# A two-layer decoder on one core: attention work reordered, two heads a PSUM bank in cross attention, MoE gathers four tiles ahead

## Reference

```
x = x + causal_attention(norm(x))            # 16 heads of 16, rotary positions
x = x + cross_attention(norm(x), context)    # 16 heads, 120 keys
x = x + PEER(norm(x))                        # product-key experts, top 10 of 8 heads
x = x + banded_attention(norm(x))            # 0.1 added to scores within 2 of the diagonal
x = x + BiDAF(norm(x), context)              # attention both ways, then W_l
x = x + MoE(norm(x))                         # 8 experts 256 -> 1024 -> 256, top 2
```

## Time and profile before

| | us |
|---|---|
| median of 3 runs | 4062.17 (4061.87 to 4063.05) |
| profiled execution | 4071.27 |
| its span, first to last instruction | 4069.5 |
| causal attention | 0 to 519 |
| cross attention | 519 to 930 |
| PEER | 930 to 2599 |
| banded attention | 2599 to 3112 |
| BiDAF | 3112 to 3389 |
| MoE | 3389 to 4069 |

### The profile page before, as it was taken

How to read it: one execution, slowest core, us unless ns; L and a number is a source line. 1 busy time by engine, 2 the same in 40 slices (tenths; PEclk the granted TensorE clock), 3 DMA queues, 4 the chain that set the end, 5 groups by cost and what they waited for, 6 DMA issues and landing times. The chain is left out here.

```text
span 4069.5 us, 98588 instructions
## 1 busy us (share of the span) xinstructions
PE 3425.7 (84%) x33488; PEld 2849.1 (70%) x33489; DVE 2980.0 (73%) x11747; ACT 1109.9 (27%) x2400; POOL 1658.6 (41%) x1626
## 2 busy tenths in 40 slices
PE   6999858784899988889999999777786886799998
PEld 4777635444788888888888888555554666688887
DVE  6778646667999999999999999499995444433332
ACT  1333424442222222222222222154442111122221
POOL 3223122212666666666666667532320000233332
PEclk8999968876999999999999999899997886799999
DMA  5344344432000000000000000244441005466665
GB/s 148 100 113 106 82 112 111 112 83 93 2 2 3 2 2 2 2 2 2 2 2 2 2 2 2 65 107 104 107 105 32 7 7 173 131 168 168 169 171 130
DMA packets 256580, 278.71 MB, mean 68 GB/s; under 512 B 43841, under 2 KB 200641, under 8 KB 255713
## 3 DMA queue, kind: packets, MB, share of 16 engines
q1 hardware_dynamic: 242401, 254.81, 22.1%
q0 software_dynamic: 13824, 19.18, 3.1%
HBM read 188.88 MB, written 72.42 MB: 64 GB/s over the span
## 5 line engine op out<-in xcount | busy, mean ns | idle before, releaser
L1129 POOL TENSOR_TENSOR peer_hot_v<-peer_hot_e,peer_parts 80x512 bf16<-80x512 bf16 x768 | 1038.1, 1378 | 505.0 <-DVE peer_hot_e L1168 504.1
L974 PE MATMUL peer_ps_u<-peer_up,peer_g 128*128 128x256 f32 x2048 | 547.9, 416 | 0.6 <-DVE x_all L1285 0.6
L955 PEld LDWEIGHTS peer_ps_h<-peer_xnT,peer_down 128*128 128x128 f32 x4096 | 511.6, 197 | 15.6
L955 PE MATMUL peer_ps_h<-peer_xnT,peer_down 128*128 128x128 f32 x4096 | 510.1, 279 | 0.0
L965 PE MATMUL peer_ps_w<-peer_hot_v,peer_hot_u 80*128 80x32 bf16 x12288 | 347.7, 177 | 177.1 <-DVE peer_g L1180 94.1
L965 PEld LDWEIGHTS peer_ps_w<-peer_hot_v,peer_hot_u 80*128 80x128 bf16 x12288 | 335.3, 97 | 204.0 <-DVE peer_hot_u L1172 109.4
L974 PEld LDWEIGHTS peer_ps_u<-peer_up,peer_g 128*128 128x128 f32 x2048 | 407.8, 208 | 55.6 <-issue 1.0
L1052 ACT ACTIVATE peer_g<-peer_ps_h 128x512 f32<-128x512 f32 x256 | 152.9, 597 | 901.9 <-PE peer_ps_h L955 901.9
L1172 DVE TENSOR_TENSOR peer_hot_u<-peer_count,peer_uvT 80x2048 bf16<-80x2048 bf16 x256 | 344.8, 1347 | 0.0
L1940 PE MATMUL moe_ps_t<-moe_xgT,moe_w 128*128 128x128 f32 x2304 | 275.3, 278 | 0.0
L1998 POOL DMA_INDIRECT moe_xg<-moe_xn_rows,moe_source x72 | 71.5, 993 | 485.7 <-DVE moe_target L2099 451.2
(11 more groups left out here) (353 smaller groups left out, 6874.2 us busy)
## 6 DMA issues: line engine op xcount, KB each, us to landing
moe_w<-in_moe_w SPq DMA_DIRECT2D x144, 512.0 KB, 4.9
causal_qs<-causal_qscratch SPq DMA_DIRECT2D x32, 384.0 KB, 3.8
cross_qs<-cross_qscratch SPq DMA_DIRECT2D x32, 384.0 KB, 3.6
band_qs<-band_qscratch SPq DMA_DIRECT2D x32, 384.0 KB, 3.9
moe_w<-in_moe_w SPq DMA_DIRECT2D x8, 1024.0 KB, 9.5
causal_qscratch<-causal_part SPq DMA_DIRECT2D x32, 192.0 KB, 2.0
causal_kscratch<-causal_part SPq DMA_DIRECT2D x32, 192.0 KB, 2.0
causal_ks<-causal_kscratch SPq DMA_DIRECT2D x32, 192.0 KB, 4.3
```

Source lines behind the costliest of these rows:

```text
L955: mm = nc.tensor.matmul(ps_h[:, n % 2, k * P:(k + 1) * P], down[:, c, 4 * n + k, :], xnT[:, par, c, :], start=(c == 0), stop=(c == DC - 1))
L974: mm = nc.tensor.matmul(ps_u[:], g[:, par, v, :], up[:, v, :], start=(v == 0), stop=(v == EV - 1))
L1129: ins = nc.gpsimd.tensor_tensor(hot_v[0:SEL, n % RING, part], hot_e[0:SEL, n % RING], w, ALU.mult)
```

## The change

In attention there are 16 probability buffers instead of 8, so that ScalarE waits for the weighing of the batch before and not for that of the same batch. Weighings come two steps later (steps 7, 11 and 15, and 3 of the next macro), the sums at 4, normalise at 7, the output projection at 11. The norm of a batch is made at step 13, three batches ahead, and the second half of `stack` stands before `turn_max` and waits only until the old heads have been read. In cross attention two heads share a PSUM bank: one instruction of VectorE and one of ScalarE treats both.

BiDAF's SyncE stores finished x tiles to the output; the MoE stage stores the last four only. In MoE there are four `xn` buffers, the w2 loads are issued behind all xn stores, the tables are made four columns at a time, there are 71 tiles and not 72, ScalarE copies the gates out of `xg`, and gathers are issued four tiles ahead and wait for `xgt_used`.

```diff
+    G = 2 if cross else 1
+    WIDE = 512 // G
...
-        probT = sb("probT", [P, 8, COLS])
+        probT = sb("probT", [P, HEADS, COLS])
...
-        PROJECT, OUT, VALUES, STACK = (2, 4, 6, 8), 10, 12, 10
-        NORMALISE = 5
+        PROJECT, OUT, VALUES, STACK, NORM = (2, 4, 6, 8), 11, 12, 10, 13
+        WEIGH, SUMS, NORMALISE = 7, 4, 7
...
                 if s > 0:
                     e.factor(b, par, s - 1)
                 if s == 0:
+                    if there(b + 1):
+                        e.stack(b + 1, 1 - par, 1)
                     if there(b - 1):
                         e.turn_max(b, par, 1)
-                    if there(b + 1):
-                        e.stack(b + 1, 1 - par, 1)
                 if there(b - 1):
-                    if s == 1:
+                    if s == WEIGH - 4:
                         e.weigh(b - 1, 1 - par, NQUAD - 1)
-                    if s == 2:
+                    if s == SUMS:
                         e.sums(b - 1, 2 * b + 2)
                     if s == NORMALISE:
                         e.normalise(b - 1, 1 - par)
-                if s % 4 == 1 and s > 1:
-                    e.weigh(b, par, s // 4 - 1)
+                if s >= WEIGH and s % 4 == WEIGH % 4:
+                    e.weigh(b, par, (s - WEIGH) // 4)
+                if s == NORM and there(b + 3):
+                    e.norm(b + 3)
                 if there(b + 2):
-                    if s == 0:
-                        e.norm(b + 2)
                     if s == 1:
                         e.turn(b + 2, par)
...
+            e.norm(2)
...
-                    settle(parts_out, OUTS * (b + 1))
+                    if c == 0:
+                        settle(parts_out, OUTS * (b + 1))
+                    else:
+                        settle(s2_done, HEADS * (b - 1))
...
-                    wait(pe, nmax_ready, HEADS * b + h - 1)
+                    if h % G == 0:
+                        wait(pe, nmax_ready, HEADS * b + h - G)
                     for q in range(TT):
                         c0, n = qcol[q], seen[q]
-                        mm = nc.tensor.matmul(ps_1[:, h % 2, c0:c0 + n], qs[0:ROWS, par, h, q * P:(q + 1) * P],
+                        mm = nc.tensor.matmul(ps_1[:, h // G % 2, h % G * WIDE + c0:h % G * WIDE + c0 + n], qs[0:ROWS, par, h, q * P:(q + 1) * P],
                                               ks[0:ROWS, par, h, 0:n], start=True, stop=not rope)
...
-                    mm.then_inc(s1_done, 1)
+                    if h % G == G - 1:
+                        mm.then_inc(s1_done, G)
...
-                    wait(pe, p_ready, HEADS * b + h - 1)
+                    if h % G == 0:
+                        wait(pe, p_ready, HEADS * b + h - G)
...
-                    mm.then_inc(s2_done, 1)
+                    if h % G == G - 1:
+                        mm.then_inc(s2_done, G)
...
-                                                  probT[0:KN, h % 8, kcol[k]:kcol[k] + S - qfrom[k]],
+                                                  probT[0:KN, h, kcol[k]:kcol[k] + S - qfrom[k]],
...
+                    if h % G < G - 1:
+                        return
                     act.wait_ge(s2_done, HEADS * b + h + 1)
-                    wait(act, pv_done, NQUAD * b + h // 4 - 1)
-                    nc.scalar.activation(probT[0:KN, h % 8, :], ps_2[0:KN, h % 2, 0:COLS], ACT.Exp).then_inc(p_ready, 1)
+                    if h % 4 == G - 1:
+                        wait(act, pv_done, NQUAD * (b - 1) + h // 4 + 1)
+                    nc.scalar.activation(probT[0:KN, h + 1 - G:h + 1, :],
+                                         ps_2[0:KN, h // G % 2, :].rearrange("p (g n) -> p g n", g=G)[:, :, 0:COLS],
+                                         ACT.Exp).then_inc(p_ready, G)
...
+                    if h % G < G - 1:
+                        return
...
-                        ins = nc.vector.tensor_reduce(nmax[:, :, h],
-                                                      ps_1[:, h % 2, 0:TT * KS].rearrange("p (q k) -> p q k", q=TT),
+                        both = ps_1[:, h // G % 2, :].rearrange("p (g n) -> p g n", g=G)[:, :, 0:TT * KS]
+                        ins = nc.vector.tensor_reduce(nmax[:, :, h + 1 - G:h + 1].rearrange("p q g -> p g q"),
+                                                      both.rearrange("p g (q k) -> p g q k", q=TT),
                                                       AX.X, ALU.max, negate=True)
-                    ins.then_inc(nmax_ready, 1)
+                    ins.then_inc(nmax_ready, G)
...
+            rows = d["out"][0:TOKENS, :].rearrange("(t p) c -> p t c", p=P)
+            def store(z, n, b):
+                sp.wait_ge(z.z_used, n + 1)
+                sp.wait_ge(loaded, 16 * NLOAD)
+                tiles = bass.ds(b * TT, TT)
+                sp.dma_start(rows[:, tiles, :], x_all[:, tiles, :]).then_inc(x_out, 16)
...
-            each(sp, [fetch])
+            for z in streams:
+                fetch(z, 0, z.k)
+            with sp.Fori(1, B // NS) as n:
+                for z in streams:
+                    fetch(z, n, NS * n + z.k)
+                for z in streams:
+                    store(z, n - 1, NS * (n - 1) + z.k)
+            sp.wait_ge(x_out, 16 * (B - NS))
...
+XN = 4
 ROW = D + E
 JT = (TOKENS * TOPE + E * (P - 1)) // P
-JT += JT % 2
...
-            tile_step(e, JT // 2 - 1, 0, forward=(True, False))
-            tile_step(e, JT // 2 - 1, 1, forward=(False, False))
-            e.result(JT // 2 - 1, 1)
+            tile_step(e, JT // 2 - 1, 0)
+            tile_step(e, JT // 2 - 1, 1, forward=(True, False))
+            tile_step(e, JT // 2, 0, forward=(False, False))
+            e.result(JT // 2, 0)
...
                 sp.wait_ge(xn_ready, g + 1)
-                sp.dma_start(rows[:, group, 0:D], xn[:, g % 2]).then_inc(xn_out[g % 2], 16)
+                sp.dma_start(rows[:, group, 0:D], xn[:, g % XN]).then_inc(xn_out[g % XN], 16)
+            tail = slice(TILES - NS * TT, TILES)
+            sp.dma_start(tiles_of(out[0:TOKENS, :])[:, tail, :], x_all[:, tail, :]).then_inc(x_out, 16)
+            for g in range(G):
                 sp.dma_start(w2[:, g:g + 1], w2_in[:, g:g + 1]).then_inc(weights, 16)
             sp.wait_ge(rw_ready, 1)
             sp.dma_start(rows[:, :, D:ROW], rw[:]).then_inc(rw_out, 16)
-            sp.dma_start(tiles_of(out[0:TOKENS, :]), x_all[:]).then_inc(x_out, 16)
...
-            last = TOPE * TILES - 1
-            for n in range(TOPE * TILES):
+            for n in range(NHOT):
                 pe.wait_ge(hot_ready, n + 1)
-                nc.tensor.matmul(ps_y[:, 0, 0:2 * JT], rowhot[:, n % HOTS, :],
-                                 tilehot[:, n % HOTS, :, :].rearrange("p a j -> p (a j)"),
-                                 start=(n == 0), stop=(n == last)).then_inc(hot_used, 1)
+                for h in range(HOTS):
+                    mm = nc.tensor.matmul(ps_y[:, 0, 0:2 * JT], rowhot[:, n % 2, h, :],
+                                          tilehot[:, n % 2, h, :, :].rearrange("p a j -> p (a j)"),
+                                          start=(n == 0 and h == 0), stop=(n == NHOT - 1 and h == HOTS - 1))
+                mm.then_inc(hot_used, 1)
...
                     wait(act, h_done, 2 * (2 * i + par - 1))
-                    nc.scalar.activation(xgT[:, par].rearrange("p c q -> p (c q)"), ps_x[:, 0:D], ACT.Copy).then_inc(xgt_used, 1)
+                    wait(act, gate_ready, 2 * i + par - 1)
+                    nc.scalar.activation(xgT[:, par].rearrange("p c q -> p (c q)"), ps_x[:, 0:D], ACT.Copy)
+                    nc.scalar.activation(gates[:, par, :], xg[:, par, D:ROW], ACT.Copy).then_inc(xgt_used, 1)
...
             def gather(j):
-                wait(pool, xgt_done, j - 1)
-                wait(pool, gate_ready, j - 1)
+                wait(pool, xgt_used, j - 1)
...
-            for j in range(3):
+            for j in range(4):
                 gather(j)
             pool.wait_ge(x_out, 16)
             for j in range(JT):
-                if j + 3 < JT:
-                    gather(j + 3)
+                if j + 4 < JT:
+                    gather(j + 4)
...
-                wait(dve, xn_out[g % 2], 16 * (g // 2))
+                wait(dve, xn_out[g % XN], 16 * (g // XN))
...
+            nc.vector.tensor_scalar(names[:, :, 0], iota[:, 0:TILES], 1.0, None, ALU.add)
+            nc.vector.tensor_copy(names[:, :, 1], pid[:].broadcast_to((P, TILES)))
...
+            steps.link(nc.vector.tensor_copy(rowb[:], slot_int[:, 1]))
+            for n in range(NHOT):
+                wait(dve, hot_used, n - 1)
+                few = slice(n * HOTS // TOPE, (n + 1) * HOTS // TOPE)
+                nc.vector.tensor_tensor(rowhot[:, n % 2], iota16[:].unsqueeze(1).broadcast_to((P, HOTS, P)),
+                                        rowb[:, few, :].rearrange("p t k -> p (t k)").unsqueeze(2).broadcast_to((P, HOTS, P)),
+                                        ALU.is_equal)
```

(66 more changed lines are left out.)

6 lines of the change are left out of this document (2 added, 4 removed).

## The result

The changed kernel takes 4083.9 us (median of 15 runs, 4073.4 to 4098.4), the kernel before 4069.8 beside it (15 runs, 4057.2 to 4080.1; the three runs shown at first gave 4062). The ratio is 1.0037, with a 95% interval of 1.0025 to 1.0048: slower by more than the 0.2% set as bound, where 1% faster was forecast.

What follows compares the result with a forecast made beforehand. No engine bounds the whole: TensorE bounds causal and MoE, VectorE band, latency cross. MoE -49, cross +7, band +7 and causal -5 sum to -40, so 4062 - 40 = 4022 us; range 3950 to 4050.

Steps and rivals of the forecast that it cites:

- cross: Cross attention stage: late moves make the period 22.55 us against 22.1, over 14 batches +7 us.
- PEER: PEER stage, 930 to 2599 us: not touched by the change, so 0.
- rival B: TensorE's clock in cross: work behind turn_max at the lower level, +4.35 us x 14 = +61, total 4083 us; chance 0.08.
- MoE: MoE stage: earlier gathers, one tile less, faster tables and four `xn` buffers, in all -49 us.
- The loop: MoE tile loop: 70 intervals of 7.24 us against 548.3 us in all, -41.5 us.
- The tables: MoE one-hot tables: 27.5 us instead of 33.2, -5.7 us, with no double rate assumed for the comparison.
- Causal: Causal attention: late moves hidden, the moved norm takes away TensorE's wait of 0.37 us, -5 us; bounds 0 and -14.
- Band: Banded attention: VectorE stalls about 0.9 us a batch and gains 0.44, +7 us; bounds -6 and +18.
- 8.65: Cross attention: us from turn_max to the next batch's first find (F0), instead of 9.84, with SyncE's waits taken off.
- 13.9: Cross attention: us from a batch's first find (F0) to turn_max, instead of 12.2.
- Rival A: Attention moves aren't late: cross period 19.5 us, cross -36 us, band -6, total 3966 us; chance 0.27.
- C: Rival, MoE gathers: they stay late because the transfer delays them, 34 us don't come, total 4056 us; chance 0.08.

Runs made afterwards that it cites:

- moves_first: Changed kernel, but in cross attention SyncE issues the last weighing's four `oq` moves ahead of the first projection's three q stores: 4035.0 us, 0.9912 of the kernel before.
- fill_wait: Changed kernel, but in cross attention TensorE does extra matmuls, results never read, just before its wait at the first turn_max: 4106.6 us, 1.0078 of the kernel before.
- pad_vector: Changed kernel plus 26 satisfied waits (14 instructions) on VectorE behind the cross stage's program: 4053.3 us, 0.9954 of the kernel before.
- moves_first_all: Changed kernel with SyncE's moves ahead of the q stores in all three attention stages, plus 14 padding instructions on VectorE behind cross: 3996.6 us, 0.9815 of the kernel before.

## Why the prediction was wrong

**The sign was decided by two terms.** Without cross and PEER the forecast was -47 and the profile shows -53.7. That the measured 4083.9 is rival B's 4083 is chance: B's stands on the 4062 of three runs, the measured one beside 4069.8; B had 61 us more than the forecast from cross alone, where 34 came, and 20 came from PEER, which B doesn't hold.

**MoE: right.** 71 results from 3563.0 to 4066.3 are 7.19 us apart (forecast 7.24), without a wait for `moe_xg`; in the earlier trace rows it was 7.72. The loop gave 45 us where 41.5 were forecast, and with it the stage gave 52.5 where 49 were forecast. The row of the results:

```profile
L2180 DVE SCALAR_TENSOR_TENSOR moe_y<-moe_ps_y,moe_gate,moe_b2w x71: 483/484/485, 3563.0 to 4066.3; 128x256 f32<-128x256 f32 x71
```

The tables took 27.5 us, as forecast against the earlier trace rows. The comparison of `rowb` with both sources in 16 bits and one of them with step 0 took 0.69 us as the one with an fp32 source did, so here trace and rule of the Trainium skill (VectorE: DVE Perf Modes, What auto-detection actually checks) agree: no double rate.

```profile
L2130 DVE TENSOR_TENSOR moe_rowhot<-moe_iota,moe_rowb x16: 685/697/712, 3512.9 to 3538.5; 128x512 bf16<-128x512 bf16 x16
```

**Causal: right**, -4.4 against -5, and in ten more profiles of the same code 1 to 6 us below the two with the code of before. **Band: mis-sized by a little.** The forecast stall of 0.9 us a batch was seen in the first batches only (0.9 to 1.95 us in four, later 0.3 at most): 0 instead of +7, the lower half of its own bounds. One profile can't tell these apart, as the same band code scatters over 13 us; the mean of the eleven is 511.9, against 513.5 and 515.2 with the code of before.

**Cross: the step that failed is "8.65" from turn_max to F0.** The mechanism was named rightly, the moves behind the three stores, and `moves_first` shows that it is the cause. From F0 to turn_max the forecast 13.9 was 14.26 in the mean of 13 batches. But from turn_max to F0 it was 10.56. Even at full clock this way takes 9.2 (`fill_wait`; 9.35 in `moves_first`), because the adds of the output, the values, the next norm and the last finds stand in VectorE's queue ahead of the second turn_max, and F0 stands behind that; I had taken SyncE's waits off a path that then was no longer SyncE's. The other 1.4 us (1.2 by the other reading above) are rival B: TensorE stands 2.8 us or more at turn_max and comes back at the lower of its levels. I gave B 0.08 and priced it at +4.35 in every batch; it came in ten of thirteen and in part. The period is 24.82 instead of 22.55: 13 x 2.3 = 30 us, and the stage's first `onT` comes 5.8 us later after the stage's start than before. Together they are the miss of 34. My argument against B, that gaps under 2 us elsewhere had full speed behind them, held nothing against a gap of 3 us, and was not even true of all short ones: behind the wait of 1.86 at 766.39 the q projection took 2.07 us, against 1.13 in the earlier trace rows. There it cost nothing that shows, as this batch went from F0 to turn_max in 14.1 us, like the others.

**PEER: the step that failed is "the change touches five of them (not the PEER stage, 930 to 2599 us)", a term put at nothing.** Its code is the same, its place is not: two heads a bank in cross take 16 instructions from VectorE's program ahead of the loop (1912 with one head, 1896 with two), and PEER lost 20 us; `pad_vector` gives them back by place alone. Nothing in the profile of before gave a price for this; the stall of 2.6 us at `x_all`, which is in both kernels, and the instruction queues' packets showed that such stalls exist.

**Rival A** (moves not late, cross -36) was right in kind: `moves_first` is that kernel, and cross gained 14 us against before (8 in `moves_first_all`). Its size was not: F0 to turn_max takes 11.86 us where A had 10.85, and the failed 8.65 is in A too (9.35 measured), so the period is 21.2 and not 19.5. C did not come.

## What to carry to other kernels

When a step is moved within a hand-written order, write down what stands ahead of its DMAs in the issuing engine's queue; here exchanging two entries of SyncE's queue turned +41 us into -14 (-8 in a second profile). Price a new wait of TensorE on the critical path with the work behind it at the lower clock as a likely case, not a remote one: here it was ten batches of thirteen. And before judging an edit that changes an engine's number of instructions, compare the stages that it doesn't touch: if one has moved, look at stalls released by "issue" and at the instruction queues, and pad the program to see whether it is the place.

## What the runs showed of the hardware

VectorE's loop of PEER (534 instructions in the profile from one turn to the next) has one stall more, 1.9 us in each turn, when it begins at instruction 1896, 2024 or 2152 of its program than when it begins at 1909, 1910 or 1912; at 1894 the stall (1.6 us) stands at `peer_hot_e`, the next instruction in the profile. A turn with it goes with one more packet of 8.2 KB on q14 (13 more in twelve turns), and takes 1 to 2 us longer than the 100.4 to 101.8 of before. That the stall is the load of instructions is inferred from these packets and from what the padding does; no view shows VectorE waiting for a packet. That the period is 128 instructions rests on the three starts and on the packets' size; which places are good, and why, stays open. The weight loads of `peer_ps_w` on TensorE stall for "issue" in the same way before and after (47.1 and 50.9 us in the same 1200 us); what this costs is not known.
